# The output projection of a Mamba chunk, moved into the first tile of the next chunk's scan

## The reference

```
xz = x @ win.T                       # 1024 -> 4096, split in u and z
u  = silu(causal_conv4(u) + bconv)
dbc = u @ wx.T                       # 2048 -> 64 + 16 + 16: dt, B, C
delta = softplus(dt @ wdt.T + bdt)
h_t = exp(delta * A) * h_{t-1} + (delta * u) * B_t     # 2048 channels x 16 states
y  = sum_n h[.., n] * C_t[n] + u * Dp
out = (y * silu(z)) @ wout.T         # 2048 -> 1024: the part that is moved
...
s = concat(fwd, flip(bwd)) @ wproj.T + bproj
g = silu(relu(xn @ Wq1.T + b1) @ Wq2.T + b2)
return x + s * g
```

## Time and profile before

| | |
|---|---|
| median of 3 runs | 6482.69 us (6480.98 to 6498.1) |
| the profiled execution, its own time | 6479.33 us |
| its span on the slowest core | 6477.6 us (other cores from 6450.9) |
| DVE busy | 4704.0 us (73%) |
| PE busy | 2758.6 us (43%), mean granted clock 0.679 |
| ACT busy | 2089.0 us (32%) |
| first instructions of emit_C for jobs 0 to 6 (top of jobs 1 to 7) | at 1160, 1855, 2567, 3256, 3956, 4650, 5343 us |
| emit_C(7) | 5964 to 6000 us |

### The profile page before, as it was taken

One profiled execution on the slowest core, in us unless ns is written; L12 is line 12 of the kernel. 1 busy time (PEld: TensorE's weight loads), 2 busy tenths in 40 slices (PEclk: granted clock), 3 DMA queues, 4 the chain that ended last, 5 costly groups with the idle time before them and its releaser, 6 DMA issues. The chain is left out here.

```text
span 6477.6 us, 35970 instructions; the slowest of 8 cores (6450.9 to 6477.6 us)
## 1 busy us (share of the span) xinstructions
PE 2758.6 (43%) x8066; PEld 921.8 (14%) x8066; DVE 4704.0 (73%) x5351; ACT 2089.0 (32%) x3260; POOL 458.2 (7%) x798
## 2 busy tenths in 40 slices
PE   2053333433343333333354445444444444334588
PEld 1010010100011001100111111111111111111233
DVE  3337888588858885888858885888588876887012
ACT  3014333333333333333333333333333343333000
POOL 0110000000000000000010000000000000000111
PEclk9975555655565556655576667666766666556799
DMA  5531111111111112111131111111111111000533
GB/s 192 154 50 43 27 23 23 46 23 25 25 46 23 23 23 49 25 23 25 25 81 34 33 33 52 33 34 37 53 33 33 33 33 46 23 22 23 141 97 109
DMA packets 152146, 303.28 MB, mean 47 GB/s; under 512 B 53616, under 2 KB 70656, under 8 KB 148864
## 3 DMA queue, kind: packets, MB, share of 16 engines
q0 software_dynamic: 88240, 241.80, 15.8%
q1 hardware_dynamic: 63696, 59.18, 2.9%
HBM read 331.35 MB, written 50.59 MB: 59 GB/s over the span
## 5 line engine op out<-in xcount | busy, mean ns | idle before, releaser
L753 ACT ACTIVATE dA_sl<-delta_sb,A_sb 128x512 bf16<-128x512 bf16 x2048 | 1309.1, 710 | 2513.1 <-DVE h_sl L809 2099.9
L824 PE MATMUL py<-h_sl,ident 128*128 128x512 bf16 x2048 | 907.9, 594 | 2632.5 <-DVE h_sl L809 2080.4
L788 DVE TENSOR_TENSOR_SCAN h_sl<-dA_sl,hcar,dBu_sb 128x512 bf16<-128x512 bf16 x1024 | 1231.6, 1265 | 28.0 <-DVE dBu_sb L770 1.8
L781 DVE TENSOR_TENSOR_SCAN h_sl<-dA_sl,hcar,dBu_sb 128x512 bf16<-128x512 bf16 x1024 | 1231.5, 1264 | 26.6
L770 DVE TENSOR_TENSOR dBu_sb<-du_sb,B_bc 128x2048 bf16<-128x2048 bf16 x512 | 625.2, 1221 | 329.0 <-ACT dA_sl L753 291.1
L824 PEld LDWEIGHTS py<-h_sl,ident 128*128 128x128 bf16 x2048 | 230.6, 127 | 3255.7 <-issue 3239.2
L539 PE MATMUL pdb<-xn_cm,wslot 128*128 128x512 bf16 x1024 | 437.5, 604 | 552.4 <-DMA wslot<-win_sl_f 276.2
L809 DVE TENSOR_TENSOR h_sl<-h_sl,C_bc 128x2048 bf16<-128x2048 bf16 x512 | 627.5, 1226 | 55.6 <-DVE hcar L798 4.5
L449 PE MATMUL pw<-xn_cm,w1f 128*128 128x512 bf16 x1024 | 404.5, 566 | 0.0
L539 PE MATMUL px<-xn_cm,wslot 128*128 128x512 bf16 x1024 | 330.0, 481 | 46.7 <-DMA wslot<-win_sl_f 46.7
L853 DVE SCALAR_TENSOR_TENSOR ytmp<-u_sil,cvec,py 128x512 bf16<-128x512 bf16 x128 | 95.7, 747 | 271.2 <-PE py L824 271.2
(11 more groups left out here) (117 smaller groups left out, 2560.7 us busy)
## 6 DMA issues: line engine op xcount, KB each, us to landing
wslot<-win_sl_f POOLq DMA_DIRECT2D x128, 256.0 KB, 4.0
wslot<-win_sl_b POOLq DMA_DIRECT2D x128, 256.0 KB, 3.7
xst<-x SPq DMA_DIRECT2D x32, 512.0 KB, 3.9
wstg<-w1t_sl POOLq DMA_DIRECT2D x8, 2048.0 KB, 9.8
wstg<-w2t_sl POOLq DMA_DIRECT2D x32, 512.0 KB, 4.2
qst<-w1t_sl POOLq DMA_DIRECT2D x64, 256.0 KB, 3.7
qst<-w2t_sl POOLq DMA_DIRECT2D x64, 256.0 KB, 3.1
h_scr<-h1st SPq DMA_DIRECT2D x128, 128.0 KB, 1.8
```

Source lines behind the costliest of these rows:

```text
L753: e.activation(out=o, in_=i, func=AF.Exp, scale=sc),
L781: e.tensor_tensor_scan(out=o, data0=d0, data1=d1, initial=i, op0=ALU.mult, op1=ALU.add),
L788: e.tensor_tensor_scan(out=o[:, ::-1], data0=d0[:, ::-1], data1=d1[:, ::-1], initial=i, op0=ALU.mult, op1=ALU.add),
L824: e.matmul(out=o, lhsT=ident[:], rhs=r, start=st, stop=sp), sPE if last else None)
```

## The change

`emit_C` is split into `emit_C_mm` (the 16 matmuls of one `dt`) and `emit_C_ev` (its eviction and transfer). Four things follow.

1. The even `dt` use `pw` as before, the odd ones use `pdb`; those who use these banks elsewhere wait for the last eviction of each.
2. The eviction is a DVE copy (`tensor_copy`) in place of the ACT copy.
3. At the top of job j only the matmuls of `dt` 0 and 1 are issued. The rest is threaded through tile 0 of the job: behind the PE sum of group g come the evictions of `dt` 2g and 2g + 1 and, for g below 3, the matmuls of `dt` 2g + 2 and 2g + 3. `emit_C(7)` at the end is not threaded, but has two banks.
4. To make room in `pw`, the `pump_h1` of tile 0, group 1 goes to tile 1, group 0. At j = 4 the load of `wout_sb` moves from the top of the job to behind tile 0.

```
@@ pump_h1, ahead of its matmuls @@
-                    wv = mk["wout_ev"].get(NKD - 1)
-                    tgt = max(pr or 0, wv or 0)
-                    if tgt:
-                        b.wait("tensor", sA, tgt)
+                    if pr:
+                        b.wait("tensor", sA, pr)
+                    wv = mk.get("pw_ev")
+                    if wv:
+                        b.wait("tensor", sV, wv)
...
@@ emit_A_mm (pdb, et == 0) and emit_dbc @@
+                pz = mk.get("pdb_ev")
+                if pz:
+                    b.wait("tensor", sV, pz)
...
@@ emit_B_et, behind the identity matmuls of group g @@
+                    cp = mk.get("cpend")
+                    if et == 0 and cp is not None:
+                        if g < 3:
+                            emit_C_ev(cp, 2 * g)
+                            emit_C_ev(cp, 2 * g + 1)
+                            emit_C_mm(cp, 2 * g + 2)
+                            emit_C_mm(cp, 2 * g + 3)
+                        else:
+                            emit_C_ev(cp, NKD - 2)
+                            emit_C_ev(cp, NKD - 1)
+                            mk["cpend"] = None
                     if g == 0 and et + 1 < NET:
                         emit_prep_v(j, et + 1)
+                    if g == 0 and et == 1 and j >= 4:
+                        pump_h1(1)
                     if g == 1:
...
-                        if j >= 4:
+                        if j >= 4 and not (et == 0
+                                           and mk.get("cpend") is not None):
                             pump_h1(1)
...
-            def emit_C(j):
+            def emit_C_mm(j, dt):
+                bank = pw if dt % 2 == 0 else pdb
+                if dt == 0:
+                    b.wait("tensor", sV, mk["gate"][(j, NET - 1)])
+                    hv = h1s["relu"].get(h1s["qe"] - 1)
+                    if hv:
+                        b.wait("tensor", sA, hv)
+                    if j > 0:
+                        b.wait("tensor", sBulkG, mk["wout_ld"])
+                if dt == 1:
+                    b.wait("tensor", sA, mk["dbc_ev"][min(j + 1, 7)])
+                pv = mk.get("pw_ev") if dt % 2 == 0 else mk.get("pdb_ev")
+                if pv:
+                    b.wait("tensor", sV, pv)
+                for et in range(NET):
...
+                mk["wout_mm"][dt] = v
+                mk["wout_last"][j] = v
+
+            def emit_C_ev(j, dt):
+                bank = pw if dt % 2 == 0 else pdb
+                b.wait("vector", sPE, mk["wout_mm"][dt])
+                if dt >= 2:
+                    b.wait("vector", sCat[dt % 2], mk["cat_dma"][dt - 2])
+                elif j > 0:
+                    b.wait("vector", sCat[dt % 2], mk["cat_dma"][NKD - 2 + dt])
+                vv = b.op("vector", lambda e,
+                          o=cstage[:, (dt % 2) * TC:(dt % 2 + 1) * TC], pb=bank:
+                          e.tensor_copy(out=o, in_=pb[:]), sV)
+                mk["wout_ev"][dt] = vv
+                if dt % 2 == 0:
+                    mk["pw_ev"] = vv
+                else:
+                    mk["pdb_ev"] = vv
+                b.wait("gpsimd", sV, vv)
+                mk["cat_dma"][dt] = b.dma("gpsimd", sCat[dt % 2],
+                    cat_scr[row0 + dt * P:row0 + (dt + 1) * P, t0:t0 + TC],
+                    cstage[:, (dt % 2) * TC:(dt % 2 + 1) * TC])
+
+            def emit_C(j):
+                emit_C_mm(j, 0)
+                emit_C_mm(j, 1)
+                for dt in range(2, NKD):
+                    emit_C_ev(j, dt - 2)
+                    emit_C_mm(j, dt)
+                emit_C_ev(j, NKD - 2)
+                emit_C_ev(j, NKD - 1)
...
@@ the loop over jobs @@
                 if j >= 1:
-                    emit_C(j - 1)
+                    emit_C_mm(j - 1, 0)
+                    emit_C_mm(j - 1, 1)
+                    mk["cpend"] = j - 1
                 if j == 4:
                     v_ms = b.op("vector", lambda e: e.memset(hcar[:], 0.0), sV)
                     emit_scan_memsets(False)
-                    mk["wout_ld"] = emit_wout_load("b", mk["wout_last"][3])
                 for et in range(NET):
                     emit_B_et(j, et)
+                    if j == 4 and et == 0:
+                        mk["wout_ld"] = emit_wout_load("b", mk["wout_last"][3])
                     if et + 2 < NET:
                         emit_delta(j, et + 2)
```

More of the change, by code:

```diff
@@ L459, in build_program @@
                 "bc_users": {}, "prep": {}, "b_dma": {},
-                "b_rest": {}, "bc_rest": {},
+                "b_rest": {}, "bc_rest": {}, "wout_mm": {},
             }
@@ L531, in emit_A_mm @@
                             (mk["zsil"].get((j - 1, NET - 1)) if et == 0 else None)
+                        pz = mk.get("pdb_ev")
+                        if pz and et == 0:
+                            b.wait("tensor", sV, pz)
                     if prev_ev:
@@ L860, in emit_B_et @@
                 mk["bc_users"][j] = mk["scan"][GG["n"] - 1]
-            def emit_C(j):
+            def emit_C_mm(j, dt):
+                s, c, half = jobs[j]
+                bank = pw if dt % 2 == 0 else pdb
[12 more added lines that the diff above has]
+                for et in range(NET):
+                    last = (et == NET - 1)
+                    v = b.op("tensor", lambda e, o=bank[:],
+                             w=wout_sb[:, et * D + dt * P:et * D + (dt + 1) * P],
+                             r=Y_sb[:, et * TC:(et + 1) * TC],
+                             st=(et == 0), sp=last:
+                             e.matmul(out=o, lhsT=w, rhs=r, start=st, stop=sp),
+                             sPE if last else None)
+                mk["wout_mm"][dt] = v
+                mk["wout_last"][j] = v
+            def emit_C_ev(j, dt):
                 s, c, half = jobs[j]
@@ L867, in emit_C @@
                 row0 = 0 if fwd else D
[L868 to L899, removed]
```

## The result

| | median | runs | ratio to before, 95% interval |
|---|---|---|---|
| before | 6490.69 us | 8 (6480.98 to 6502.94) | |
| after | 6276.14 us | 8 (6262.7 to 6312.39) | 0.9676 [0.9656, 0.9696] |

The changed kernel is 214.6 us faster. 6276 us was predicted.

A forecast was written before the change was run, and what follows sets the result against it. DVE was taken to bound the kernel inside a job, `emit_C` on PE and ACT at its top. 6479.33 - 268.7 + 31.5 + 31 + 7 - 7 = 6273, with 3.4 for the median 6276 us; range 6235 to 6325.

The forecast's parts named there:

- the stall that goes: Job tops: DVE's 41.6 us wait of the first `dBu_sb` for `dA_sl` falls to about 3.2; gain 268.7 us (242 to 276).
- evictions on DVE: Tile 0: eight new DVE copies per boundary, six in the open, cost 4.5 us each boundary, 31.5 in all (22 to 42).
- moved load at job 4: Tile 1 of job 4: `wslot` queues behind the eight `wout_sb` transfers, delaying DVE's group 2; loss 31 us, 24.5 if only the sum counts.
- projection late, jobs 5 and 6: Tile 1: late `wslot`, then moved `pump_h1`, its eviction and `dA_sl`, delay DVE by 3.5 us each, 7 in all (3 to 10).
- the same, jobs 1 to 3: Projection behind tile 0: the sum is done at X + 16.6 to 18.9, ahead of X + 20.7, and costs nothing.
- `emit_C(7)`: At the end, before the barrier: with two banks PE goes on without waiting for the copy; gain 7 us.
- the stall stays: Rival at the job tops: something else releases the first `dBu_sb`, so only the costs remain; 6545 us, chance 0.03.
- Low clock: Rival in tile 0: PE stays at its low clock, some 15 us of waiting per boundary, 105 in all; 6381 us, chance 0.12.
- taking turns: Rival in tile 0: pairs of `dt` cannot run beside DVE's group, 44 us per boundary, 308 in all; 6585 us, chance 0.03.
- The row of 6.37 us: Profile row: a `dt` takes 6.37 us where PE came from idleness, 3.61 at the fast clock; used for low clock.
- X: The end of tile 0's last product, from which the prediction timed the `wout_sb` load, `wslot`, projection and sum.
- load hidden: Rival at job 4: the `wout_sb` load costs nothing because `wslot` gets through beside it; 6245 us, chance 0.10.

## Why the prediction was right

Its terms against what core 5 shows:

| step | predicted | measured | how |
|---|---|---|---|
| the stall that goes | -268.7 | -268.1 | 290.3 at seven tops before, 22.2 after |
| evictions on DVE | +31.5 | +21.9 | tiles 0 without the first wait: 251.8, then 273.7 |
| moved load at job 4 | +31 | +27.1 | tile 1: 40.0, then 67.1 |
| projection late, jobs 5 and 6 | +7 | +7.3 | tile 1: 3.6 and 3.7 longer |
| the same, jobs 1 to 3 | 0 | +1.5 | tile 1 of job 1 |
| `emit_C(7)` | -7 | -7.3 | 35.9, then 28.7 |
| not foreseen | | +6.5 | ends of seven jobs 440.1, then 445.3; tiles 2 to 14 +1.3 |
| sum | -206 | -211 | scan part -211.2 |

**The stall.** The step that carried the forecast held, in its size and, at six of seven tops, in its releaser: `B_bc`, 3.2 us a top. The upper end, job 0's 7.01, came at no top. The rival *the stall stays* has nothing left.

**The evictions** are the term that was mis-sized most, 4.5 us per boundary against 3.1. The step between two copies is 0.60 us, not 0.66. And the sum was taken at 1.87 or 1.03 us without asking which: at the higher clock it is 1.03, so the wait at the end of the tile is 1.28 in place of 2.12, filled by the last two copies. Six copies of 0.60, less 0.84, and 0.33 of waiting for `pdb` (0.80, 1.07 and 0.44 in jobs 1, 2 and 4, over seven) give 3.1. In all that is at the prediction's lower bound, 22, which was put for another case, the old wait of 2.12 filled whole. The Trainium skill, "VectorE: DVE Perf Modes", section "The TRN2 errata", led to an estimate of 0.66 us for this copy; the trace has 0.68, and what counts for a queue of them is 0.60.

**Low clock, and taking turns.** The granted clock in tile 0 is 0.88 and 0.93, and there are three waits of a copy for PE, 2.3 us in all. The section on PSUM-queue depth-cycling of the Trainium skill's "TensorE: Matmul & The Clock Gate" warns of a clock that swings when a kernel cycles through banks with short pauses. Two banks in turn, with sums between them and pauses of 0.9 to 1.7 us, did not do that here: from the second sum of tile 0 on the granted clock is 1.00 in all seven jobs. The row of 6.37 us that the prediction set beside this warning is another case, one bank and a pause of 5.38 us. Where PE came to the first sum from 7.7 to 8.0 us of idleness, in jobs 1, 2 and 4, that sum took 1.87 us, and these are the three jobs in which a copy waits.

**The load at job 4.** The mechanism is as put: the first `wslot` is behind the eight transfers, and the run with the load behind the projection takes the loss back. The sum was 4 us too long: PE gets `wslot` at X + 29.7 (X is 3174.5) where 32.5 was predicted, and the `pump_h1` takes 1.89 us, not 3.3. The gap was predicted ahead of group 2; 16.23 us of it stand a group earlier, since the quantizer's signs on ACT are behind the eviction of `px`. The rival *load hidden* falls.

**The projection.** For jobs 5 and 6 the chain and its price were right. For jobs 1 to 3 the step "is ahead of X + 20.7 and costs nothing" failed in job 1: there X is 1180.74, and `wslot` was issued at 1185.37, X + 4.6 and not X + 2.5, because POOL stood still for 2.43 us ahead of its second `cat_scr`; it did so on every core, and in no other job (0.05 to 0.64 there). PE's second projection ends at X + 20.4, the sum behind it, and DVE waits 1.82 us for that sum. What held POOL for the 2.43 us is not shown by the trace.

The sum of the terms was near because the load and the evictions were both dearer in the sum than on the chip, by 13.5 us, and 8 us that were not foreseen came on top. Of these, 5 us lie at the ends of the jobs; core 1 has them too (437.7 and 442.4). Most of it stands at one wait, that of the next job's first `delta_sb` for PE's `pd`: over the seven ends 72.4 us before and 76.7 after, and longer on seven of the eight cores. Why it should be longer stays open; one such end differs by 2 to 3 us between two executions of the same kernel.

That the median came out at the very 6276 us is luck. Those two errors nearly cancel, and the forecast went out from 6482.69 us, where eight runs of the kernel before have 6490.69: it was of 207 us less, and 214.6 less was measured.

## What to carry to other kernels

When work is threaded into another engine's busy stretch, follow each in-order queue past the new place, transfers as well: here the threading itself did what it should, and all that was lost, 36 us, was lost in POOL's and ACT's queues, and issuing three things at other places (a load, a `pump_h1`, a first `wslot`) brought it back. Put the new copies on the engine that has room, if what stands behind them in its program can be issued ahead. And a wait of the bound engine for a short piece of another engine's work is worth a look at that engine's clock: 121 waits of 2.12 us looked like a fixed latency, and some 0.83 of nearly each was the sum at the lower clock, as PE came from idleness.

## What the hardware did that was not expected

- Four matmuls of the same form took 1.86 us after 9.5 us of idleness (granted clock 0.50) and 1.03 us when they came 1.8 us after a run of 15 others (1.00); such runs, whose results nobody reads, in 121 tiles took 1.6% off the kernel (ratio 0.9585 to 0.9433).
- Two DVE copies from PSUM in a row start 0.60 us apart though each is recorded with 0.68.
- A `wslot` of 256 KB issued right behind the eight transfers to `wout_sb` let PE go on 21.1 us after its issue (3183.12 to 3204.22); issued ahead of them, 5.8 us after (3198.99 to 3204.75, in the run with the load behind the projection).
